# A graph network's edge stage: a constant row copied into PSUM by ScalarE for one of two banks, and six gather buffers with a wait at every third unit

## What is computed

```python
h   = relu(layernorm(x))                                  # node features, gathered by src
pol = clip(edge_attr[:, 0:1], 0, 1)
e   = relu(raw @ W_e1.T + b_e1) @ W_e2.T + b_e2           # raw: 64 features of an edge
emb = (e * (pol + 0.01)) @ W_le.T + b_le
msg = relu(h[src] + emb)
agg = segment_sum(msg, dst)
out = x + (relu(layernorm((h + agg) @ W_g1.T + b_g1) * g + b)) @ W_g2.T + b_g2
```

## Time and profile before

| | us |
|---|---|
| median of three runs | 2294.32 |
| the profiled execution | 2291.79 |
| its span, first to last instruction | 2290.1 |

### The profile page before, as it was taken

The page is one execution under the profiler, slowest core; times in us unless marked ns, Lnnn a source line. Parts: engine busy times, 40 slices in busy tenths (PEclk is TensorE's granted clock), DMA queues, the critical chain, the costliest instruction groups (busy, mean ns, idle before and its releaser), DMA issues. The chain is left out here.

```text
span 2290.1 us, 45615 instructions
## 1 busy us (share of the span) xinstructions
PE 2220.2 (97%) x14665; PEld 2021.1 (88%) x14665; DVE 2143.2 (94%) x4129; ACT 1881.2 (82%) x4267; POOL 1706.5 (75%) x1671
## 2 busy tenths in 40 slices
PE   3899999999999999999999999999999999999988
PEld 3799999999999999999999999999999999999887
DVE  8899999999999999999999999999999999999888
ACT  6788888888888888888888888888888888888754
POOL 7677777777777777777777777777777777777672
PEclk9899999999999999999999999999999999999989
DMA  9466666666666666666666666666666666666342
GB/s 301 133 158 151 154 152 153 152 153 152 153 152 154 152 153 153 153 153 152 154 151 153 152 152 153 154 152 155 150 154 151 156 150 155 151 153 152 99 132 95
DMA packets 138613, 349.58 MB, mean 153 GB/s; under 512 B 34113, under 2 KB 60674, under 8 KB 138370
## 3 DMA queue, kind: packets, MB, share of 16 engines
q0 software_dynamic: 77376, 211.39, 34.6%
q1 hardware_dynamic: 60994, 135.21, 24.9%
HBM read 333.64 MB, written 12.82 MB: 151 GB/s over the span
## 5 line engine op out<-in xcount | busy, mean ns | idle before, releaser
L537 POOL DMA_INDIRECT hx<-gather_table,sidx x1612 | 1601.7, 994 | 498.5 <-issue 474.1
L691 PE MATMUL bank<-wcr,hh 128*128 128x256 f32 x3224 | 904.6, 281 | 0.0
L690 PE MATMUL bank<-wcr,hh 128*128 128x256 f32 x3224 | 903.3, 280 | 0.0
L692 PE MATMUL bank<-wcr,hl 128*128 128x256 f32 x3224 | 903.2, 280 | 0.0
L615 DVE SCALAR_TENSOR_TENSOR bank<-bank,gt,hx 128x256 f32<-128x256 f32 x1612 | 698.9, 484 | 88.7 <-PE bank L692 86.4
L554 ACT ACTIVATE mhl<-bank 128x512 fp32r<-128x512 f32 x806 | 483.1, 599 | 308.1 <-PE bank L704 187.5
L691 PEld LDWEIGHTS bank<-wcr,hh 128*128 128x128 f32 x3224 | 606.3, 188 | 36.8
L690 PEld LDWEIGHTS bank<-wcr,hh 128*128 128x128 f32 x3224 | 609.2, 189 | 18.1
L692 PEld LDWEIGHTS bank<-wcr,hl 128*128 128x128 f32 x3224 | 605.9, 188 | 0.0
L625 DVE SCALAR_TENSOR_TENSOR mhl<-bank,mhl 128x512 fp32r<-128x512 f32 x806 | 519.2, 686 | 12.6
L604 DVE SCALAR_TENSOR_TENSOR hl<-bank,hh 128x512 fp32r<-128x512 f32 x806 | 514.8, 679 | 4.4 <-ACT hh L548 4.1
(11 more groups left out here) (112 smaller groups left out, 1173.4 us busy)
## 6 DMA issues: line engine op xcount, KB each, us to landing
raw<-in_attrT SPq DMA_DIRECT2D x402, 256.0 KB, 4.7
hx<-gather_table,sidx POOLq DMA_INDIRECT x1612, 2.9
x_sba<-in_x SPq DMA_DIRECT2D x12, 512.0 KB, 9.6
gather_table<-x_sba SPq DMA_DIRECT2D x12, 512.0 KB, 6.8
u_x<-in_x SPq DMA_DIRECT2D x12, 512.0 KB, 8.7
out<-u_x SPq DMA_DIRECT2D x12, 512.0 KB
dst_i<-in_dst_m SPq DMA_DIRECT2D x1, 805.5 KB
sidx<-in_src_m SPq DMA_DIRECT2D x1, 805.5 KB
```

What stands on the lines that cost most here:

```text
L537: eng.indirect_dma_start(out=hx[:, u % NX, j, :], out_offset=None, in_=tables, in_offset=bass.IndirectOffsetOnAxis(ap=sidx[:, t:t + 1], ax ...
L690: eng.matmul(o, hh[:, u % 2, k, e0:e0 + P], wcr[:, 0, k, :], start=False, stop=False)
L691: eng.matmul(o, hh[:, u % 2, k, e0:e0 + P], wcr[:, 1, k, :], start=False, stop=False)
L692: last = eng.matmul(o, hl[:, u % 2, k, e0:e0 + P], wcr[:, 0, k, :], start=False, stop=(j == 1 and k == 1))
```

## The change

In units 2 to 402 the bank of q = 1 is no longer opened by the matmul L685. ScalarE copies the constant row, now kept on all 128 partitions, into both halves of that bank, after its onehot(u+1) and before message_high(u, 0), and the twelve matmuls add to what it wrote. TensorE waits for that copy (`r_sd`), and the wait for message_low moves from TensorE to the copy. The gathers have six buffers in place of four, and GpSimd waits at every third unit only, then for the buffers of three units at once. To have the constant row on all partitions, the setup computes it with 128 columns of b_e2 in place of one. Semaphores of the node loads are shared by two paths, of which one is taken.

```diff
-NX = 4
+NX = 6
+NW = 3
...
-        c2 = sb("c2", [1, D])
+        c2 = sb("c2", [P, D])
...
                 for m in range(2):
-                    last = eng.matmul(bank[1][0:1, 0:D], be2[:, m:m + 1], wle[:, m, :],
+                    last = eng.matmul(bank[1][:, 0:D], be2[:, m:m + 1].broadcast_to([P, P]), wle[:, m, :],
                                       start=(m == 0), stop=(m == 1))
...
-                link(eng.tensor_copy(c2[:, :], bank[1][0:1, 0:D]))
+                link(eng.tensor_copy(c2[:, :], bank[1][:, 0:D]))
...
                     for u in range(UNITS):
-                        if u >= NX:
-                            eng.wait_ge(r_t, 2 * (u - NX) + 2)
+                        if u >= NX and u % NW == 0:
+                            eng.wait_ge(r_t, 2 * (u + NW - 1 - NX) + 2)
...
+                    def seed(u):
+                        eng.wait_ge(r_ml, 2 * (u - 2) + 2)
+                        eng.copy(LB[(2 * u + 1) % 4][:, :].rearrange("p (j n) -> p j n", j=2),
+                                 c2[:, :].rearrange("p (a n) -> p a n", a=1).broadcast_to([P, 2, D])).then_inc(r_sd, 1)
...
                         if u + 1 < UNITS:
                             onehot(u + 1)
+                            if u >= 1:
+                                seed(u + 1)
                         message_high(u, 0)
...
                         for q in range(2):
-                            if u >= 2:
-                                eng.wait_ge(r_ml, 2 * (u - 2) + q + 1)
-                            eng.matmul(LB[(2 * u + q) % 4][:, :], onr[:, :], c2w, start=True, stop=False)
+                            if u >= 2 and q == 0:
+                                eng.wait_ge(r_ml, 2 * (u - 2) + 1)
+                            seeded = u >= 2 and q == 1
+                            if seeded:
+                                eng.wait_ge(r_sd, u - 1)
+                            else:
+                                eng.matmul(LB[(2 * u + q) % 4][:, :], onr[:, :], c2w, start=True, stop=False)
```

## The result

The changed kernel takes **2256.93 us**, median of 4 runs (2254.22 to 2267.95), against 2293.34 for the kernel before, measured beside it. The ratio is 0.984, 95% interval 0.980 to 0.988. The forecast was 2235, range 2208 to 2264: faster, by 36 us in place of 58. The profiled execution took 2254.22 us, 37.6 less than the one of before; the forecast for it was 2232.3.

A forecast was written before the change was run, and what follows sets the result against it. TensorE was taken to bound the kernel at 5.199 us a unit; afterwards gathers at 5.005 plus 0.04 of holds give 5.045, so 399 x (5.194 - 5.045) = 59.5 us saved: 2235 us, range 2208 to 2264.

The forecast's parts named there:

- What bounds the kernel before: Edge stage: TensorE sets the pace at 5.199 us a unit, four gathers on GpSimd want 5.005, 96% of it.
- L407 holds gathers: VectorE's subtraction with both inputs in SBUF holds a gather whose row begins inside it, by 0.56 us at most.
- (a) The matmul: TensorE, units 2 to 402: one of two L685 matmuls goes, saving 0.235 us, so its unit becomes 4.964.
- (b) The copy: ScalarE's added copy takes 0.51 us a unit, making ScalarE 4.44 + 0.51 = 4.95; its wait costs nothing.
- (c) The buffers: GpSimd's gathers: six buffers and a wait at every third unit, taken as worth 0.
- What is late next, and the hold: After the change gathers set the pace: 5.005 us a unit plus 0.04 for a 0.45 hold every 11 units, 5.045.
- Chained waits: Rival: four engines within 0.09 us of each other pass on late hand-overs; 5.12 a unit, 2262 us; chance 0.12 (5.09 to 5.165).
- TensorE stays the bound: Rival: the 0.30 us between gathers shrinks, so TensorE's 4.964 a unit rules; 2200 us; chance 0.05.
- L407 locked onto the gathers: Rival: wrong-length landings put VectorE's subtraction onto a gather's start every time; 5.285 us a unit, 2328 us; chance 0.07.
- Dear seed: Rival: ScalarE's copy takes over 0.757 us; at 1.28 a unit is 5.72, 2502 us in all; chance 0.03.
- Clock: Rival: small idle gaps drop TensorE to the 1.2 GHz level in one of ten units; 2395 us; chance 0.01.
- What was to show it: Signs: TensorE idle about 0.08 us a unit, first matmuls 5.0 apart, gather pitch 1.25, long rows once in ten units.

The follow-up runs named there:

- short raw_low: The changed kernel with VectorE's raw_low subtraction (L407) on 8 of 512 columns from unit 4 on: 2216.1 us, ratio 0.967.
- three gathers of four: The changed kernel with one gather in four left out from unit 6 on: 2206.2 us, ratio 0.959.

## Why the prediction was right, and where its size was off

- **What bounds the kernel before.** TensorE, with GpSimd's gathers at 96% of it: shown. With the matmul gone, the gathers' 5.005 is what a unit can't go below (short raw_low, 5.003), and with a gather gone as well TensorE's is next (2206 for 2200, 4.97 a unit for 4.964).
- **L407 holds gathers.** Shown from three sides: every held gather started while an L407 ran and ended 0.81 to 0.84 after it, in every trace; with it shortened there is one left, behind one of the first, still full-length L407s; in another form, with the same inputs, there are as many. What is argued only is that its two inputs in SBUF are the cause; that instructions with one input in PSUM hold nothing supports it, and no run put one of this instruction's inputs elsewhere. The forecast had the hold go one way only, and held every gather whose row begins inside L407. Both are off at the edge: a gather that starts less than 0.044 after L407 goes free and lengthens it by up to 0.08, as at 850.83, while an L407 that begins 0.06 after a gather's start, as at 1003.71, takes its 0.69.
- **(a) The matmul**, 0.235 a unit: its worth was real (short raw_low and three gathers of four needed it), and 0.095 of it arrived.
- **(b) The copy**, 0.51: measured at 0.52, its row 0.59 to 0.61. Its wait was covered: no run's waits name it. TensorE waits for the copy only where there are two. The 4.44 for the rest of ScalarE was the step that failed here. It was taken as the unit less the idle time, and a row may start before the one ahead of it has ended, so idle time counts less than the free room. From pitches the rest is 4.13 in a unit without a window (4.65 - 0.52). The forecast had ScalarE's idle time fall to near 0.1 a unit; on VectorE alone it waits 83.9 us in 373 units, 0.23. VectorE's 4.92 was near (4.82 by pitches, and for the windows two instructions of 0.33 in seven units, 0.09: 4.91). With a right count ScalarE would have stood well apart from the other three.
- **(c) The buffers**: 0, shown from both sides.
- **What is late next, and the hold.** This term is the miss. Forecast 0.04 a unit, measured 0.092. The size of one hold was right, 0.45 foreseen and 36.5 / 91 = 0.40 found; its frequency was not, once in 11 units against 401 / 91 = 4.4. The step was "TensorE feeds it at 4.93": VectorE walks at 4.80 in a unit without a window, because, as it seems, every wait for a landing gives TensorE a lead. Reckoned afterwards with that, seven units gain 7 x 5.005 - (7 x 4.81 + 2 x 0.33) = 0.71, 0.10 a unit, and the forecast's walk of 0.48 takes 4.7 units: 0.45 / 4.7 = 0.096 a unit, 5.10 in all, and 2291.8 - 399 x 0.093 = 2254.7 us, against 2254.2 measured. That this comes so near is in part luck: the walk of 0.48 was taken from one pair of rows, and it depends on where a slow landing puts L407. The early rows of the trace of before, 5.09, had it, and were named as a bound.
- **Rivals.** Chained waits: out (three gathers of four; more work on VectorE is faster). TensorE stays the bound: out; the gap of 0.30 was the same in every kernel, wherever GpSimd didn't wait. L407 locked onto the gathers: its mechanism, a landing of the wrong length that puts L407 onto a gather's start, is the one at work, but in one unit of 4.4 and at half the price from which it would have ended slower. Dear seed: out. Clock: the granted clock stayed at 1.00 with 12 us idle in 1000.
- **What was to show it.** Gaps of TensorE 0.06 a unit for 0.08; its first-layer matmuls 4.95 apart in most pairs of units for 5.0, with the gaps in the others; gathers at a pitch of 1.25; long rows not once in ten units and at any of a unit's places but once in 4.4 and nearly always at the last, since it is the one whose slow landing sets where L407 restarts.

## What to carry to other kernels

When two engines share something and run at nearly the same pace, ask which gains on which: the one held loses its whole hold if it is the slower of the two, and nothing if it is the faster, so 0.12 us a unit of more work on the right engine was worth 20 to 26 us here. A saving on the bounding engine is worth what the next pace allows, and that is read from start-to-start pitches, not from busy shares or idle sums. Where an engine waits for a landing, look also at which other load was issued just before it. A forecast of a coupled loop should use the rows of a stretch in which the new order already ruled, here the first five units, before any reasoning about its speed.

## What the runs showed of the hardware that wasn't expected

- A gather of 128 rows of 1 KB costs GpSimd 0.947 + 0.305 us where nothing holds it, the same to 0.01 in every kernel, with a satisfied wait in front or none.
- A gather whose row starts 0.044 to 0.5 us after the start of the VectorE instruction on two SBUF inputs (L407, 0.69 us) ends 0.82 after that instruction's end, up to 0.5 late. One that starts earlier, from 0.03 before L407 to 0.044 after it, keeps its 0.95, and L407 lasts up to 0.77. VectorE's instructions with an input in PSUM keep their length and hold nothing.
- A gather whose row ends less than 2 us after an issue of raw features (two DMAs of 256 KB) lands 3.6 to 3.7 us after its row's end in the median, the others about 1.8.
- A VectorE write of 48 columns between two long instructions costs about 0.01 of time though its row says 0.10; one of 168 columns costs 0.12.
- ScalarE's copy of 128x512 from SBUF into PSUM has a pitch of 0.52, and its four 128x128 instructions with a bias 0.29 each.
